# Query products moved from the cross-attention tiles into a stage of four token groups, and the cross loop laid out in four like steps per tile

## The reference, cut to what matters

```python
q = hidden_states @ Wq                      # hidden_states: the normalized x
k = encoder_hidden_states @ Wk
v = encoder_hidden_states @ Wv
scores = jnp.einsum('bhsd,bhkd->bhsk', q, k) * scale
probs = jax.nn.softmax(scores, axis=-1)
out = jnp.einsum('bhsk,bhkd->bhsd', probs, v)
out = out @ Wo + bo
```

## Time and profile before

| | us |
|---|---|
| median of 3 runs | 1826.18 |
| lowest, highest | 1825.54, 1827.83 |
| the profiled execution's own time | 1826.2 (it is its span) |
| PE busy, its weight loads busy | 1732.6, 1486.9 |
| DVE, ACT, POOL busy | 1242.4, 676.8, 309.9 |

### The profile page before, as it was taken

The page is one execution under the profiler, slowest core; times in us unless marked ns, Lnnn a source line. Parts: engine busy times, 40 slices in busy tenths (PEclk is TensorE's granted clock), DMA queues, the critical chain, the costliest instruction groups (busy, mean ns, idle before and its releaser), DMA issues.

```text
span 1826.2 us, 41682 instructions
## 1 busy us (share of the span) xinstructions
PE 1732.6 (95%) x15355; PEld 1486.9 (81%) x15367; DVE 1242.4 (68%) x3118; ACT 676.8 (37%) x1471; POOL 309.9 (17%) x183
## 2 busy tenths in 40 slices
PE   6899999999999999999999999899999999996778
PEld 6788988988988988988889888798989898973333
DVE  4767667667677676676676676477868686656686
ACT  3334334334334334334344443322222222213556
POOL 3312212122122122112122121100000000000334
PEclk8999999999999999999999999999999999997899
DMA  5110110110101101001101002501110101003002
GB/s 204 33 35 26 35 43 26 34 39 30 34 29 40 34 29 34 32 30 39 34 26 43 29 26 82 185 29 46 40 57 30 57 29 36 17 23 114 32 16 92
DMA packets 45218, 84.46 MB, mean 46 GB/s; under 512 B 3904, under 2 KB 20352, under 8 KB 45184
## 3 DMA queue, kind: packets, MB, share of 16 engines
q1 hardware_dynamic: 45184, 84.01, 14.0%
HBM read 71.41 MB, written 12.58 MB: 46 GB/s over the span
## 4 chain that ended last, share of the span: by engine, by line
PE 54%; issue 32%; DVE 8%; ACT 4%; POOL 1%; DMA 1%; DVEq 0%; SPq 0%; ACTq 0%; POOLq 0%
PE psum_o L537 15%; PE psum_s L505 10%; PE psum_q L464 6%; PE psum_t L551 5%; PE psum_o L563 5%; PE psum_s L475 3%; PE psum_t L485 3%; PE psum_q L475 2%; PE psum_o L1209 2%; PE psum_s L1209 2%; DVE nmax L799 2%; DVE oT L791 1%; DVE qk L695 1%; PE psum_t L523 1%; ACT probs L652 1%
## 5 line engine op out<-in xcount | busy, mean ns | idle before, releaser
L505 PE MATMUL psum_s<-cT,qk 128*128 128x258 f32 x2304 | 319.1, 289 | 10.7 <-ACT probs L652 7.5
L537 PE MATMUL psum_o<-pT,c_nat 128*128 128x512 f32 x1152 | 312.4, 407 | 0.0
L505 PEld LDWEIGHTS psum_s<-cT,qk 128*128 128x128 f32 x2304 | 292.9, 191 | 23.6 <-ACT probs L652 15.2
L863 POOL TENSOR_TENSOR c_nat<-c_raw,zero 128x768 fp32r<-128x768 f32 x64 | 93.9, 1467 | 870.6 <-PE psum_o L537 521.3
L652 ACT ACTIVATE probs<-psum_s,nmax 128x257 f32<-128x257 f32 x256 | 122.0, 476 | 312.7 <-DVE nmax L799 312.7
L537 PEld LDWEIGHTS psum_o<-pT,c_nat 128*128 128x128 f32 x1152 | 202.5, 188 | 41.4 <-DVE oT L791 0.3
L791 DVE SCALAR_TENSOR_TENSOR oT<-p_last,c_last,psum_o 128x512 f32<-128x512 f32 x192 | 142.8, 744 | 44.2 <-PE psum_o L537 30.6
L799 DVE TENSOR_REDUCE nmax<-psum_s 128x1 f32<-128x257 f32 x256 | 107.3, 419 | 88.6 <-PE psum_s L505 86.4
L695 DVE TENSOR_TENSOR pT<-psum_t,pT 128x512 fp32r<-128x512 f32 x128 | 86.3, 685 | 54.1 <-ACT pT L633 54.1
L464 PE MATMUL psum_q<-xnT,wq 128*128 128x128 f32 x1024 | 123.0, 280 | 0.0
L464 PEld LDWEIGHTS psum_q<-xnT,wq 128*128 128x128 f32 x1024 | 120.5, 197 | 0.0
(11 more groups left out here) (180 smaller groups left out, 2878.1 us busy)
## 6 DMA issues: line engine op xcount, KB each, us to landing
c_raw<-in_ctx_dram SPq DMA_DIRECT2D x64, 384.0 KB, 3.2
out_dram<-x_out SPq DMA_DIRECT2D x32, 256.0 KB, 2.0
x_ln<-in_x_dram SPq DMA_DIRECT2D x16, 256.0 KB, 2.7
x_res<-in_x_dram SPq DMA_DIRECT2D x16, 256.0 KB, 3.2
x_ln<-out_dram SPq DMA_DIRECT2D x16, 256.0 KB, 2.8
x_res<-out_dram SPq DMA_DIRECT2D x16, 256.0 KB, 2.9
x_all<-out_dram SPq DMA_DIRECT2D x1, 4096.0 KB, 15.7
out_dram<-o_sb SPq DMA_DIRECT2D x16, 256.0 KB, 2.0
```

The lines of the kernel that those rows point to most:

```text
L505: i = pe.matmul(ps[:, 0:SKP], qk[:, part, rg, c, b, :], cT[b % 2][:, moving, c, :], start=n == 0, stop=n == 3 * KC - 1)
L537: i = pe.matmul(ps[:], c_nat[b % 2][:, part, k, cols], pT[:, moving, k, :], start=n == 0, stop=n == 5)
L863: G.tensor_tensor(c_nat[i][:, 0, :, :].rearrange("p k n -> p (k n)"), c_raw[:].rearrange("p k n -> p (k n)"), zero[:].to_broadcast([P, 2 * ...
```

## The change

1. **A project stage ahead of the cross loop.** Four groups of 4 tiles (512 tokens). For a group: x normalized and transposed, both split in two parts; q in eight products of 12 float32r matmuls with 512 columns (before: 32 float32 matmuls of 128 columns per tile); q·Wk in 8 x 3 x 2 banks of 3 float32r matmuls with 512 columns. ACT and DVE copy those banks whole to `staged` (4 slots), and SP stores each slot to a new array in DRAM, `qk_dram`: 8 stores of 2 x 786,432 bytes per group, in rows of 1536 bytes, 50.3 MB over the four groups. Wq and Wk are split in two parts at the start.
2. **In the cross loop** the query product of a tile is loaded from DRAM into `raw` (24,576 bytes of each partition) and split there: ACT makes the high part and DVE the low part in four pieces of 1536 elements, all in the step of batch 3 of the tile before. The x transposes, layer norms, `pe_q` and `pe_qk` are gone from it.
3. **Four like steps.** Batch 3's probabilities and PV products move into batch 0 of the next tile, and Wv and Wo of a tile into batch 1 of the next, Wo between two PV products. The scores have three banks (`s0, s1, q0, s0`). Two of four scalings of the probabilities go to ACT, and so do the last key and its scalars. `c_raw` has two buffers.
4. **Behind the last tile** a tail: transposes, PV, Wv and directly behind it Wo.
5. Wo is split in tile 0 by ACT and DVE (before: by POOL). Wv, Wo and bo are loaded when the last slot is stored, since they lie where the slots were.

```diff
+        def pe_group_q(pe, s, j):
...
             for k in range(KD):
+                for part, moving in PARTS:
+                    m = pe.matmul(ps[:], wq[:, part, k, j * P:(j + 1) * P], xnT[:, moving, k, :, :],
...
+        def pe_group_qk(pe, s, j):
+            taken(pe, project(("Q", s, j)))
...
+            for c in range(KC):
+                places = [empty(pe, project(("QK", s, j, c, par))) for par in range(2)]
+                for part, moving in PARTS:
+                    for par in range(2):
+                        r = slice(64 * par, 64 * par + 64)
+                        m = pe.matmul(places[par][0][:], wkT[r, part, j, c * P:(c + 1) * P], qT[r, moving, j, :, :],
...
+        def pe_project_all(pe):
+            pe_group_x(pe, 0)
+            for s in range(GROUPS):
+                for j in range(4):
+                    pe_group_q(pe, s, j)
+                    if (s, j) == (0, 1):
+                        pe_start_weights(pe)
+                for j in range(4):
+                    pe_group_qk(pe, s, j)
+                for j in range(4, 8):
+                    pe_group_q(pe, s, j)
+                if s < GROUPS - 1:
+                    pe_group_x(pe, s + 1)
...
+                for j in range(4, 8):
+                    pe_group_qk(pe, s, j)
...
+        def pe_cross_tile(pe, t, section):
+            begun, more = section != "first", section != "last"
             for b in range(4):
+                before = begun or b > 0
+                pe_scores(pe, t, b, 0, section)
+                if before:
+                    pe_probsT(pe, t, b, section)
+                pe_scores(pe, t, b, 1, section)
+                if b == 1 and begun:
+                    pe_wv(pe, t, 0, section)
+                pe_scores(pe, t, b, 2, section)
+                if before:
+                    pe_probs_last(pe, t, b, section)
+                if b == 1 and begun:
+                    pe_wv(pe, t, 1, section)
+                pe_scores(pe, t, b, 3, section)
+                if before:
+                    pe_pv(pe, t, b, 0, section)
+                if more or b < 3:
+                    pe_ctxT(pe, t, b, section, (0, 1))
+                if before:
+                    pe_pv(pe, t, b, 1, section)
+                if b == 1 and begun:
+                    pe_wo(pe, t, section)
+                if more or b < 3:
+                    pe_ctxT(pe, t, b, section, (2,))
+                if before:
+                    pe_pv(pe, t, b, 2, section)
```

DVE's order in the cross loop, and its new low part of the query product (`qk_next` holds in batch 3, save in the last tile; `scale` on ACT does `rg` 0 and 1):

```diff
+        def dve_qk_low(dve, t, rg, section=None):
+            if section:
+                full(dve, U1(("S", 3, rg), t - 1, section))
+            dve.wait_ge(s_qhi, 4 * t + (rg + 1))
+            part = [qk[:, i, rg, :, :, :].rearrange("p c b (h q) -> p h (c b) q", h=4) for i in range(2)]
+            nc.vector.tensor_tensor(part[1], raw[:, rg, :, :].rearrange("p h (a q) -> p h a q", q=SQ), part[0].bitcast(F32),
+                                    ALU.subtract).then_inc(s_qlo, 1)
...
+                row_max(b, 3)
+                inverse(b, 2)
+                if qk_next:
+                    dve_qk_low(dve, t + 1, 0, section)
+                if before:
+                    dve_attended(dve, t, b, 0, section)
+                inverse(b, 3)
+                if qk_next:
+                    dve_qk_low(dve, t + 1, 1, section)
+                if after:
+                    ctxT(b, 0)
+                    ctxT(b, 1)
+                norm(b, 2)
                 norm(b, 3)
...
+                if before:
+                    dve_attended(dve, t, b, 1, section)
+                if b == 1 and begun:
+                    dve_x_out(dve, t, section)
+                if after:
+                    ctxT(b, 2)
+                if qk_next:
+                    dve_qk_low(dve, t + 1, 2, section)
+                if before:
+                    dve_attended(dve, t, b, 2, section)
+                if qk_next:
+                    dve_qk_low(dve, t + 1, 3, section)
```

SP in the project stage and at the head of a tile:

```diff
+                for j in range(8):
+                    for c in range(KC):
+                        for par in range(2):
+                            taken(sp, project(("QK", s, j, c, par)))
+                    for par in range(2):
+                        sp.dma_start(qk_dram[GROUP * s:GROUP * (s + 1), :, 2 * (j // 4) + par, j % 4, :].rearrange("t p n -> p t n"),
+                                     staged[:, j % 4, par, :, :]).then_inc(s_staged[j % 4], 16)
+            for i in range(4):
+                sp.wait_ge(s_staged[i], 64 * GROUPS)
+            sp.dma_start(wv[:], Wv.rearrange("(k p) n -> p k n", p=P)).then_inc(s_wvo, 16)
+            sp.dma_start(wo_raw[:], Wo.rearrange("(k p) n -> p k n", p=P)).then_inc(s_wvo, 16)
...
+        def sp_cross_tile(sp, t, section):
...
+                if more or b < 2:
+                    sp.wait_ge(s_nat, 4 * t + (b + 1))
+                    load_ctx(sp, 4 * t, b + 2)
+                if b == 0:
+                    sp.wait_ge(s_qlo, 4 * t + 4)
+                    if more:
+                        load_qk(sp, t, 1)
```

More of the change, by code:

```diff
@@ L539, in pe_pv @@
-            i.then_inc(filled[bk], 1)
-        def pe_wv(pe, t, n, last):
+                    taken(pe, U1(("PT", b, k), t, section))
+                pe.wait_ge(s_nat, 4 * t + b)
+            ps, done = empty(pe, U1(("PV", b, m), t, section))
+            for k in range(2):
+                for part, moving in PARTS:
+                    i = pe.matmul(ps[:], c_nat[(b - 1) % 2][:, part, k, m * P:(m + 1) * P], pT[:, moving, k, :],
+                                  start=(k, part, moving) == (0, 0, 0), stop=(k, part) == (1, 1))
@@ L660, in act_cross_tile, with ctxT @@
+            def ctxT(b, c):
+                act_high(act, U1(("CT", b, c), t, section), cT[(b + 1) % 2][:, 0, c, 0:2 * P], cols(2 * P))
             for b in range(4):
+                before, after = begun or b > 0, more or b < 3
                 exp(b, 0)
-                if b:
-                    act_probsT(act, t, b - 1, last)
+                if before:
+                    for k in range(2):
+                        act_probsT(act, t, b, k, section)
+                if b == 3 and more:
+                    act_qk_high(act, t + 1, 0)
@@ new lines, in act_cross_tile, with act_cross_tail @@
+                act_last_scalars(act, b, 4 * t)
+                if after:
+                    ctxT(b, 2)
+                if b == 3 and more:
+                    act_qk_high(act, t + 1, 2)
+                    act_qk_high(act, t + 1, 3)
+                if section == "first" and b in (1, 2):
+                    act_wo_high(act, b - 1)
+        def act_cross_tail(act):
+            t, section = TILES, "tail"
+            for k in range(2):
+                act_probsT(act, t, 0, k, section)
+            act_probs_last(act, t, 0, section)
+            for n in range(2):
+                act_wv(act, t, n, section)
@@ L716, in build_kernel, with dve_low, project_low @@
+        def dve_low(dve, place, split, out, high, in_):
+            bk, _ = place
+            dve.wait_ge(copied[bk], split[1] + 1)
+            nc.vector.tensor_tensor(out, in_(bank[bk]), high.bitcast(F32), ALU.subtract).then_inc(drained[bk], 1)
+        def project_low(dve, unit, out, high, in_):
+            dve_low(dve, project(unit), SPLIT1(unit, 0, "project"), out, high, in_)
         class Chain:
@@ new lines, in sp_cross_tile @@
+        def sp_cross_tile(sp, t, section):
+            begun, more = section != "first", section != "last"
+            for b in range(4):
+                if more or b < 2:
+                    sp.wait_ge(s_nat, 4 * t + (b + 1))
+                    load_ctx(sp, 4 * t, b + 2)
+                if b == 0:
+                    sp.wait_ge(s_qlo, 4 * t + 4)
+                    if more:
+                        load_qk(sp, t, 1)
+                    else:
+                        load_w2(sp, "q")
+                if b == 1 and begun:
+                    sp_x1(sp, t, section)
+                    sp.dma_start(x_res[:], rows(x_rows, t)).then_inc(s_xres, 16)
+            if not more:
+                taken(sp, U1(("S", 3, 3), t, section))
+                for name in "kvo":
+                    load_w2(sp, name)
```

1060 lines of the change are left out of this document (574 added, 486 removed).

## The result

The changed kernel takes **1854.38 us** (median of 4 runs, 1853.13 to 1854.94) against 1826.3 for the kernel before, measured beside it: ratio 1.0154, 95% interval 1.014 to 1.0169. It is slower by 28 us, the forecast was 12.5. The side was right, the time lies in the range, and the size was off by more than the forecast change itself. The profiled run of after has an own time of 1853.13 and a span of 1851.3 (from the first to the last instruction).

The account below looks back on a forecast made before the run. PE was taken to bound the loop, busy 98.55 of 100 us. Stage 196, tile 0 28.2 + 2.5 + 16, loop 15 x 60.2, end 5.8 + 687.2 sum to 1838.7; forecast 1839 us, 0.7% slower, range 1795 to 1880.

Parts of the forecast that it names:

- The project stage: Ahead of the cross loop: 42 us per group, first scores at 196 us if the stores keep up.
- sign of being wrong in the stage: Project stage: the prediction called itself wrong there if the scores begin below 185 or above 210 us.
- q·Wk in half rows: Project stage: half-row matmuls run side by side at 0.12 us each; rival, not side by side, 1903 us in all.
- Tile 0: First scores to batch 3 of the first tile: 28.2 for steps, 2.5 for splitting Wo, 16 for a context stall.
- The batch of the pieces: Loop's batch 3: 13.2 us of DVE work in a 10.7 us step makes PE 3.9 us late.
- Without GpSimd's part: Loop: a tile of 57.7 us, 1801 us in all; the rival that the steps hold had chance 0.26.
- With GpSimd's part: Loop: POOL's split delays the last pieces, lag 6.3 us, a tile of 60.2 us.
- sign for the main step: Loop: the prediction called its main step wrong if the tile is below 59 us.
- the -10.0 of the table: Loop, the term of 15 tiles: predicted 903 us at 60.2 each, measured 893.0.
- PE's idle time: Loop: almost all in batch 0, ahead of the fourth scores and the first PV product.
- The rule: Loop: VectorE instructions with two SBUF inputs and GpSimd instructions reading SBUF exclude each other; tile 60.2 instead of 57.7 us.
- The end: From the last tile's batch 3 on: 5.8 us, then 687.2 us (685 to 692) left as before.

Follow-up runs that it names:

- e1: The changed kernel with the next x load issued behind the first eight of the 16 stores, not behind all: 1833.65 us.
- e3: The changed kernel with GpSimd's split of the next tile's first context waiting for the fourth low piece; x load still late: 1832.9 us.
- e7: The changed kernel with the edits of e1 and e3 together: 1809.11 us.
- e4: The changed kernel with VectorE's four low pieces cut to 128 of 1536 elements, the rest left out: 1799.12 us, a single run.
- e11: The changed kernel with e1's edit and the fourth low piece behind the next tile's first row maximum, without GpSimd's wait: 1812.88 us.
- e9: e7 with the fourth piece in the next tile, batch 2's context requested ahead of the weights, the second piece behind two context parts: 1782.58 us.
- e8: e7 with batch 2's context requested ahead of the weights and the fourth low piece on GpSimd behind VectorE's third: 1795.64 us.

## Why the prediction was wrong, and where it was right

- **The project stage is the step that failed** ("42 us per group ... 196, if the stores keep up"). The stores kept up: groups are 42.2 us apart in e1 and the scores begin at 197.48. What failed is what the stage's sum left out. It bounded the stores' rate and counted the bytes of the next x, but never placed that load in SP's written order behind the 16 stores, nor VectorE's wait for it ahead of the copies. That is two stalls of 9.3 and 9.7 us and half-clock matmuls behind them; without them (e1) the scores begin 20.7 us sooner. The prediction's sign of being wrong in the stage, scores above 210, has come.
- **q·Wk in half rows**: three groups of six start 0.68 apart, 0.113 each, against 0.12 taken and 0.232 for one with all rows; the two halves run side by side. The first q product starts at 18.71 (18.6), q·Wk at 36.96 (36.6).
- **Tile 0** came near (44.1 against 46.7) by misses of opposite sign. The stall for the context is 7.7 us against 13.6 taken. The first step takes 11.9 us instead of 6.8, with small waits (1.2, 0.6 and 1.5 us) and the low clock in it. The low halves of Wo (2.99 and 3.88 us on VectorE; 2.5 of delay for PE was put down in this term) fall into the first of the 15 tiles: PE waits 2.94 and 4.32 there, and batches 3 and 0 take 33.8 where later ones take 26.1.
- **The batch of the pieces**: the hand-written order held. Pieces end 8.0, 10.5, 14.9 and 17.8 us behind the first scores at 328.36 (predicted 8.1, 10.5, 15.0 and 17.3, or 19.7 behind GpSimd). Without GpSimd's part 57.7 was predicted, and e3 and e7 show 57.8. That sum hides small errors: the two batches lose 4.5 us against plain ones in e3, not 3.9, and plain ones take 10.48, not 10.7. With GpSimd's part 60.2 was predicted: every third tile shows 60.5, and there the last two pieces end 16.0 and 19.3 us behind the first scores (by the prediction, 16.1 and 19.7). The rest shows 58.4 to 58.6. The prediction put GpSimd first in every tile; the 0.67 us by which the last PV products come later at the lower clock turn the order round. Its own sign for the main step, a tile below 59, is met by ten of the 14 tiles, though the mean, 59.06, is just above. 15 x (60.2 - 59.06) = 17.1 too much, less the 7.1 by which the first tile, with Wo's halves, is longer than the mean (66.1), is the -10.0 of the table. It hid half of the miss in the stage, which is luck.
- **PE's idle time** in the loop was forecast almost all in batch 0. The largest sum is in batch 3 instead, 1.9 us per tile ahead of the third context transpose (the row of 32.3 us): the prediction's own working had this wait, its list of signs did not.
- **The rule** of the Trainium skill, page "SBUF — State Buffer", section "Who interferes with whom", was taken against a row of 0.7 us only. The trace agrees for instructions of 1.5 to 3.5 us; e3 takes the overlap away, e4 shortens one side, and e11 puts it back.
- **The end** came 3.0 later than the 693.0 carried over. The same work behind the last Wv took 1.3 to 6.1 us less in the other runs than in after, so this is no more than their spread; no run takes it apart. The 1.8 of own time beyond the span comes, as far as the record shows, from how before was counted and not from the change.

What stays open: why e3 has one tile of 59.3 among those of 57.8 (e7 has it too, at the same place), why PE's clock falls in some tiles and not in others, and how much of e4's tile is ScalarE's.

## What to carry to other kernels

When a stage is moved behind a queue of stores, write down that queue in its issued order and put each load at its place in it: a rate that fits says nothing of a load that stands behind 16 stores, and an engine that waits for it in order stops everyone that it serves. Work packed anew on VectorE is not free because VectorE is busy for only 64% of the span: place it where VectorE waits for other engines, and keep GpSimd's SBUF work away from VectorE's instructions with two SBUF operands by a wait on the last of them. The change itself was sound: with its loads early, GpSimd held back and two pieces moved (e9), it is 2.4% faster than before instead of 1.5% slower.

## What the runs showed of the hardware

- The exclusion of VectorE and GpSimd is per instruction and goes to whoever starts first: a VectorE instruction of 0.29 us took 1.36 behind a GpSimd one of 1.47. VectorE instructions with one operand in PSUM ran beside GpSimd's 3.47 at their own 0.68 to 0.69 (e8).
- A faster TensorE went with a slower tile: where the last PV products took 1.64 us and not 2.31 to 2.91, GpSimd started first, and the tile took 60.5 instead of 58.4 to 58.6. With GpSimd held back (e3) the tile took 57.8 with either.
- GpSimd's subtraction of 1536 elements takes 3.47 us where VectorE's takes 1.75.
- The stores of 768 KB ran at 359 to 375 GB/s in windows of 4 us with a DMA share of 1.03 to 1.04 (after, 44 to 56 and 98 to 110), inside the bounds of 311 and 417 taken for them.
